# A decoder layer's hand-off from attention to experts: the last tiles' turns written out, five experts' weights loaded a turn sooner, identity products in TensorE's waits

## The reference

```
x = x + self_attention(layernorm(x))                   # causal, rotary, 16 heads
x = x + cross_attention(layernorm(x), ctx)             # q and output projections on int8-rounded values
x = x + experts(layernorm(x))                          # top 8 of 64 experts, 128 places each
```

## Time and profile before

| | |
|---|---|
| median of 3 runs | 1581.28 us (1580.71 to 1584.12) |
| the profiled execution | 1576.11 us |
| its span, first to last instruction | 1574.3 us |
| PE, DVE, ACT, Pool busy | 90%, 72%, 62%, 43% of the span |
| granted TensorE clock, mean | 0.963 of full |
| DMA packets | 195.68 MB |

### The profile page before, as it was taken

The page is one execution under the profiler, slowest core; times in us unless marked ns, Lnnn a source line. Parts: engine busy times, 40 slices in busy tenths (PEclk is TensorE's granted clock), DMA queues, the critical chain, the costliest instruction groups (busy, mean ns, idle before and its releaser), DMA issues.

```text
span 1574.3 us, 35702 instructions
## 1 busy us (share of the span) xinstructions
PE 1423.6 (90%) x11060; PEld 1074.5 (68%) x11060; DVE 1134.7 (72%) x3075; ACT 971.0 (62%) x3345; POOL 673.4 (43%) x655
## 2 busy tenths in 40 slices
PE   3689999999999999999999999999728888888895
PEld 2467777777777777777777777777516555555563
DVE  5568888888888888888888888888633444444453
ACT  3357777777777777777777777777614333333332
POOL 1012443534444434535344444344542545455556
PEclk9799999999999999999999999999859999999997
DMA  8771332222211110101100111100497999999964
GB/s 297 302 262 35 117 134 105 98 105 81 91 39 38 41 34 27 27 28 33 45 28 27 27 33 39 35 21 22 134 368 203 288 266 292 273 288 280 261 99 50
DMA packets 159882, 195.68 MB, mean 124 GB/s; under 512 B 39685, under 2 KB 122117, under 8 KB 159824
## 3 DMA queue, kind: packets, MB, share of 16 engines
q1 hardware_dynamic: 120912, 157.14, 30.4%
q0 software_dynamic: 38912, 37.87, 11.8%
HBM read 127.47 MB, written 130.29 MB: 164 GB/s over the span
## 4 chain that ended last, share of the span: by engine, by line
PE 66%; DMA 23%; issue 5%; DVE 3%; ACT 2%; POOL 1%; SPq 1%; POOLq 0%; DVEq 0%
PE bank L507 34%; DMA out<-x,slots 20%; PE bank L532 7%; PE bank L489 7%; PE bank L525 5%; PE bank L539 4%; PE bank L513 3%; PE bank L545 2%; PE bank L520 2%; DMA x_in<-in_x 1%; ACT probs L972 1%; PE bank L494 1%; POOL routed L1754 1%; DMA probsT<-in_kT_w 1%; DMA probsT<-in_oT_w 1%
## 5 line engine op out<-in xcount | busy, mean ns | idle before, releaser
L972 ACT ACTIVATE probs<-bank,small 128x128 f32<-128x128 f32 x1024 | 362.4, 378 | 51.2 <-DVE small L1276 47.9
L1754 POOL DMA_INDIRECT routed<-row,slots x248 | 253.4, 1022 | 132.8 <-issue 73.0
L1719 POOL TENSOR_TENSOR small<-small,half 128x1 f32<-128x1 f32 x96 | 54.5, 567 | 534.3 <-DVE small L1248 534.3
L1825 POOL DMA_INDIRECT out<-x,slots x128 | 198.6, 1551 | 193.3 <-DMA out<-x,slots 144.9
L972 ACT ACTIVATION_READ_ACCUMULATOR probs<-bank,small 128x1 f32 x1024 | 222.0, 217 | 0.0
L966 ACT ACTIVATE probsT<-bank 128x512 f32<-128x512 f32 x256 | 144.1, 612 | 102.3 <-PE bank L532 102.3
L1276 DVE TENSOR_REDUCE small<-bank 128x4 f32<-128x512 f32 x256 | 166.8, 683 | 32.3 <-PE bank L525 32.3
L532 PE MATMUL bank<-idf,probs 128*128 128x128 f32 x1024 | 146.6, 277 | 1.9 <-ACT probs L972 1.9
L1674 DVE TENSOR_SCALAR slots<-pairs 128x1 uint32<-128x1 f32 x128 | 13.7, 149 | 180.4 <-DMA out<-x,slots 176.8
L532 PEld LDWEIGHTS bank<-idf,probs 128*128 128x128 f32 x1024 | 122.0, 144 | 25.1 <-DVE probs L1285 3.0
L1206 ACT ACTIVATE xn<-bank 128x192 f32<-128x192 f32 x64 | 21.3, 332 | 149.3 <-PE bank L912 149.3
(11 more groups left out here) (244 smaller groups left out, 3845.7 us busy)
## 6 DMA issues: line engine op xcount, KB each, us to landing
w_gate_up<-in_w_gate SPq DMA_DIRECT2D x128, 192.0 KB, 3.6
w_gate_up<-in_w_up SPq DMA_DIRECT2D x128, 192.0 KB, 3.8
w_down<-in_w_down SPq DMA_DIRECT2D x128, 192.0 KB, 4.1
routed<-empty_row SPq DMA_DIRECT2D x4, 5120.0 KB, 22.8
x_in<-in_x SPq DMA_DIRECT2D x32, 256.0 KB, 2.6
ctx_sb<-in_ctxT_in SPq DMA_DIRECT2D x32, 256.0 KB, 3.0
x_res<-in_x SPq DMA_DIRECT2D x32, 256.0 KB, 2.6
out<-x SPq DMA_DIRECT2D x32, 256.0 KB, 2.0
```

The lines of the kernel that those rows point to most:

```text
L972: last = act.activation(probs[:, g, j * P:(j + 1) * P], bank[:, b, j * P:(j + 1) * P], ACT.Exp, bias=negated[:, h:h + 1], **({"accum_out": ...
L1754: pool.indirect_dma_start(routed, bass.IndirectOffsetOnAxis(ap=slots_of(m)[:, k:k + 1], axis=0), row_of(m)[:, :], None, bounds_check=SLOTS ...
L1825: pool.indirect_dma_start(out.rearrange("b p (h c) -> (b p h) c", h=2), bass.IndirectOffsetOnAxis(ap=place_of[k % 2][:, half_:half_ + 1], ...
```

## The change

Three edits, in the last turns alone.

On SP, three experts are loaded after `body(B+1)`, as soon as q, k and v of tile 32 are projected, and two after `body(B+2)`, with no further wait; the rest comes after `body(B+4)` as before, from the sixth expert on, and the wait for p_xk and p_o moves there.

On PE, turns B+3 to B+5 are written out. Up to `cross_scores(32)` the order is the same. After it `turn_cross_probs_1(32)` stands ahead of `turn_normed(31)`, `logits(31)` behind `turn_cross_probs_0(32)`, and `positions(31)` behind the four weighings of tile 32. Five groups of identity products are added (`keep_warm`): 6, 10, 18, 8 and 56 products of an identity matrix with itself repeated, written to banks 3 and 7, whose results nobody reads and which wait for nothing.

On ACT, turn B+4 is written out with one step moved: `router_exp(31)` behind `copy_cross_probs_2(32)`. (`copy_cross_probs_3` is then behind it.) DVE and Pool are unchanged.

```diff
@@ sync
             for cur in range(B + 1, B + 6):
                 body(cur)
+                if cur == B + 1:
+                    for projected in (p_q, p_k, p_v):
+                        sp.wait_ge(projected, 3 * B)
+                    for k in range(3):
+                        load_weights(k, k)
                 if cur == B + 2:
-                    for projected in (p_q, p_k, p_v, p_xk, p_o):
-                        sp.wait_ge(projected, 3 * B)
-                    for k in range(2):
+                    for k in range(3, 5):
                         load_weights(k, k)
                 if cur == B + 4:
-                    for k in range(2, 8):
+                    for projected in (p_xk, p_o):
+                        sp.wait_ge(projected, 3 * B)
+                    for k in range(5, 8):
                         load_weights(k, k)
@@ tensor
+            def keep_warm(b, count):
+
+                ones_and_zeros = idf[:, :].bitcast(BF16)
+                for _ in range(count):
+                    pe.matmul(bank[:, b, :], ones_and_zeros[:, 0:P],
+                              ones_and_zeros.unsqueeze(1).to_broadcast([P, 2, 2 * P]), start=True, stop=True)
@@ tensor
-            for cur in range(B + 1, B + 6):
+            for cur in (B + 1, B + 2):
                 body(cur)
+            positions(B - 2)
...
+            cross_output(B - 1)
+            cross_scores(B)
+            keep_warm(3, 6)
+            turn_cross_probs_1(B)
+            turn_normed(B - 1)
+            turn_cross_probs_2(B)
+            turn_cross_probs_0(B)
+            logits(B - 1)
+            turn_cross_probs_3(B)
+            weigh_cross_1(B)
+            weigh_cross_3(B)
+            weigh_cross_0(B)
+            weigh_cross_2(B)
+            positions(B - 1)
+            turn_cross_attention(B)
+            keep_warm(7, 10)
+            turn_quantised_o(B)
+            cross_output(B)
+            keep_warm(7, 18)
+            turn_normed(B)
+            logits(B)
+            keep_warm(7, 8)
+            positions(B)
+            keep_warm(7, 56)
@@ scalar
-            for cur in range(B + 1, B + 6):
+            for cur in (B + 1, B + 2, B + 3):
                 body(cur)
+            cross_exp_1(B)
+            ffn_normed(B - 1)
+            cross_exp_2(B)
+            copy_normed(B - 1)
+            cross_exp_3(B)
+            copy_cross_probs_2(B)
+            router_exp(B - 1)
+            copy_cross_probs_3(B)
+            copy_cross_probs_1(B)
+            copy_cross_probs_0(B)
+            copy_turned_attention(B)
+            copy_quantised_o(B)
+            body(B + 5)
```

More of the change, by code:

```diff
@@ L895, in _ @@
                 body(cur)
-            for cur in range(B + 1, B + 6):
+            for cur in (B + 1, B + 2):
                 body(cur)
+            positions(B - 2)
+            weigh_cross_1(B - 1)
+            weigh_cross_3(B - 1)
+            weigh_cross_0(B - 1)
+            weigh_cross_2(B - 1)
+            turn_cross_keys(B)
+            turn_cross_attention(B - 1)
+            cross_values_b(B)
+            turn_quantised_x(B)
+            cross_values_c(B)
+            cross_values_a(B)
+            cross_queries(B)
+            turn_quantised_o(B - 1)
+            turn_cross_queries(B)
+            cross_output(B - 1)
[22 more added lines that the diff above has]
+            keep_warm(7, 56)
             def turn_rows(n, k, use):
```

## The result

| | median us | lowest to highest |
|---|---|---|
| before | 1582.48 | 1578.61 to 1589.61 |
| after | 1588.75 | 1582.74 to 1593.65 |

These are 22 runs of each kernel on the same chip. The ratio after to before is 1.0036, with an interval from 1.0025 to 1.0046: 4.0 to 7.3 us slower. The forecast was 1580.4 with a range up to 1583.5; the median lies above it. The profiled execution of after took 1586.08 us around a span of 1584.3, against 1576.11 and 1574.3.

The account below looks back on a forecast made before the run. The expert stage cannot start before the last row of `routed` lands, so only the chain through 1118 to 1183 us was costed. Terms 0.0 - 0.2 - 0.7 + 0 = -0.9 us, from 1581.28, gave 1580.4 us, range 1575.5 to 1583.5.

Parts of the forecast that it names:

- Five experts loaded a turn sooner ... Cost nothing.: SP's queue: the earlier weight loads delay nothing, as tile 29's store still lands 7 us early; cost 0.
- meeting of two paths for tile 32: At `ffn_power(32)` on Pool: tile 32's cross attention and tile 31's scatters arrive within half a microsecond.
- the sum: All terms from tile 31's release to the expert stage: 0.0 - 0.2 - 0.7 + 0 = -0.9 us.
- Rival 3: Loads a turn earlier make tile 29's store or tile 32's context land late: +1 to +3 us, 1583; chance 0.03.
- The store out of the way, -1.4: `second_sum(31)`: tile 30's store has no load ahead, so TensorE releases it at 1128.2 instead of 1129.64.
- The scores' clock, -0.5: `cross_scores(32)` on TensorE: a shorter idle stretch before it may keep the clock up; -0.5 us, bounds 0 and -0.9.
- The order, +1.9 to the first scatter of 31: TensorE: `logits(31)` and `positions(31)` stand behind tile 32's cross work, delaying tile 31's first scatter by 1.9 us.
- `ffn_power(32)` stays behind Pool's scatters: Pool runs in order, so it stays at about 1157.2 and the cross part's gain ends in a wait there.
- The products, -0.2: Identity products in TensorE's waits, mainly around tile 32's last turn, logits and positions: -0.2 us, bounds -1.35 and +1.0.
- The landing, -0.7: Last scatter before the expert stage lands sooner, as loads end about 12 us sooner: -0.7 us, bounds 0 and -1.1.
- The start of the expert stage, 0: First experts' work on TensorE: full clock would save 1.8 us, a later rise costs up to 1.5; taken 0.
- The first rival: TensorE's clock stays up through the stretch: -4.4 to -6.5 us, about 1576; chance 0.25.

Follow-up runs that it names:

- late_five_only: Kernel before with only SP's loads changed: first five experts loaded after turn B+3's store, once tile 29's scatters have landed; ratio to before 0.9975.
- late_five: Changed kernel with the first five experts loaded after turn B+3's store, once tile 29's scatters have landed; ratio to before 0.9977.
- split_no8: `late_five` with `ffn_power(32)` behind the fifth of tile 31's eight scatters and without the eight identity products before `positions(32)`; ratio to before 0.9961.
- sp_only: Kernel before with the change's SP edit alone, TensorE and ScalarE as before; ratio to before 1.0024.
- three_early: Kernel before with three experts loaded after `body(B+1)` and two after `body(B+3)`, behind tile 29's scatters; on another chip, ratio to before 1.0004.
- split: `late_five` with `ffn_power(32)` put behind the fifth of tile 31's eight scatters; ratio to before 0.9960.

## Why the prediction was wrong, step by step

**The step that failed** is the first one: "Five experts loaded a turn sooner ... Cost nothing." It checked the queue that the loads were moved in (SP's) and the landings of the transfers behind them, and both were right: the store of tile 29 was no cause of anything. It did not look at what else uses the DMA engines at that time. Eight indirect DMAs of Pool stand there, and the timeline of before shows a 2.90 us "issue" gap in them that no semaphore explains. The rows shown of Pool began at 1146, two turns after. The loads put a DMA share of 1.06 where it had been nearly idle, as a stretch of each kernel's pause shows, after and then before:

```profile
1103.00:1104.00 1.00, 0.86 (x6) 0.63 (x7) 0.96 (x4) 1.00 (x6) 0.15 (x1) 1.00 1.06 393
```

```profile
1096.00:1097.00 1.00, 1.00 (x9) 0.68 (x8) 1.00 (x2) 1.00 (x7) 0.00 (x0) 1.00 0.06 9
```

With the pause 4.0 us longer, `ffn_power(30)` went from being ready together with its input to 3.6 us behind it (input 1108.15, start 1111.77). I had noted this very meeting of two paths for tile 32 and not for tile 30. In the terms of the sum: "Cost nothing" was 0 and measured +6.5 us at `attT_lo` of 31, of which 3.0 are the pause and 3.6 the step. Rival 3 named the right edit and the wrong place: it asked whether a store or a context would land late, and gave it 0.03.

**The rest of the sum**, by distances in after, came out as follows.

- *The store out of the way, -1.4*: right. -1.39 alone, in `late_five_only`. In after the difference falls only from 6.53 to 5.63, -0.9; the half clock on the return from the 5.75 us wait (0.56 at 1118) lies in this stretch.
- *The scores' clock, -0.5*: the hole shrank to 1.66 us as said, and the scores took 1.17 us, the full clock. -0.92, the far bound.
- *The order, +1.9 to the first scatter of 31*: +1.4. `logits(31)` ran at half clock as taken (1.80).
- *`ffn_power(32)` stays behind Pool's scatters*: right, as VectorE's wait shows. In after its input was ready at 1161.49, 2.5 us before its start, and VectorE stood for it:

```profile
1161.34 0.15 DVE L1311 TENSOR_SCALAR small<-small 128x1 f32<-128x1 f32 x1
...
1164.62 0.27 DVE L1316 TENSOR_SCALAR small<-small 128x1 f32<-128x1 f32 x1 [3.13 <-POOL small L1782]
```

- *The products, -0.2*: of the wrong sign, within the bounds. The eighteen left a hole of 3.86 us, the clock was at half in tile 32's turn, and eight products took 3.29 us at a place with room for 2.44. From the logits' start to `positions(32)` it is 4.89 us against 4.41, so +0.5.
- *The landing, -0.7*: 2.09 us against 3.12, -1.03:

```profile
1184.62 2.09 DMA routed<-row,slots
```

- *The start of the expert stage, 0*: +1.2. The first experts' products took 4.98 us at half clock, against 4.14. The last filler block ends more than 4 us before them.

Without the failed step the sum would have had the right sign and been too small. `late_five`, which is the change with the loads put where they meet no pause, has -2.7 us of distance and -3.6 by its ratio, where the sum was -0.9. That isn't the merit of order and products: `late_five_only` has the same without them. The first rival, the clock up throughout, came about in no run. `late_five`, with the same 98 products as after (I wrote 100 in the forecast), was at full clock from the scores to 1155.5 and then at half until 1165.7; it fell within the 4.86 us that TensorE stood idle behind its wait for Pool. In `split_no8`, where that wait was short, the clock was up in tile 32's last turn and logits, but at half from 1136.8 to 1140.2 and again from 1160.7 to 1164.1.

## What to carry to other kernels

Before transfers are moved to a quiet stretch, look at what is quiet about it: list everything that issues or uses DMAs there, on every queue, and any "issue" gap in it, for a gap that no semaphore explains may grow with the traffic. A trace that keeps single packets can tell what such a gap lasts for. Then look where two engines arrive at one instruction within half a microsecond, one turn back and one turn on, not only in the turn that is edited: such a meeting hides no delay at all. And if a reorder's gain ends in a wait on an engine that runs in order, move the step on that engine too; here three scatters put behind `ffn_power(32)` took 1.7 us off the distance in one execution of each, where reorder and products together had taken none (103.30 against 103.32).

## What the runs showed of the hardware that I had not expected

- Pool pauses 2.9 us ahead of two scatters, and they are the same two in all fourteen kernels. With the DMA engines saturated by plain transfers the pause is 6.77 to 7.06 us, in five kernels, with traffic over a part of it 5.07. It ends 2.12 to 2.58 us after the last packet of the scatter ahead of it, in every trace. Five more indirect DMAs ahead of it don't move it.
- The 80 small packets of a scatter were through 0.78 us behind it with the DMA engines quiet, and 3.8 to 4.7 us behind it beside saturating weight loads (tile 31 in before; the second scatter of tile 29 in after and `sp_only`).
- A 128x1 step of VectorE took 3.72 us beside an unbroken row of Pool's elementwise instructions, in four kernels, and 0.16 with Pool held back for 1.02 us. In `three_early` it took 2.37 us, ending at 1313.58 with Pool's instruction (1312.27 + 1.28 = 1313.55).
- The same products in the same order did not keep the same clock: `logits(31)` took 1.00 us in `late_five` and 1.81 in `split`, whose TensorE programs don't differ up to there. One execution doesn't tell what a filler is worth.
